# The adjacency is handed over with its last two axes swapped, and the gates' stage reads its tiles as loaded

## What is computed

```
h = relu(layernorm(x))
x_conv = conv branch of h (17 taps)
A   = exp(-dist(s, s)) * adj              # s = h @ w_se.T + b_se, 3 wide
msg = relu(h @ w_msg.T + b_msg)
x_nmp[n] = sum over m of A[n, m] * msg[m]
r, z, n = gates of [x_conv, x_nmp] and h  # the n gate: tanh(gi_n + r * gh_n)
x = x + (1 - z) * n + z * h
h2 = relu(layernorm(x))
out = x + relu(h2 @ w[:d] + (adj @ h2) @ w[d:] + bias)
```

## Time and profile before

| | us |
|---|---|
| median of 3 runs | 2045.76 |
| lowest and highest | 2044.67, 2048.74 |
| the profiled execution | 2044.45 |
| its span | 2042.6 |
| TensorE busy (matmuls) | 1902.4, 93% |
| VectorE busy | 1483.0, 73% |
| ScalarE busy | 797.3, 39% |
| POOL busy | 378.3, 19% |

### The profile page before, as it was taken

How to read it: one execution, slowest core, us unless ns; L and a number is a source line. 1 busy time by engine, 2 the same in 40 slices (tenths; PEclk the granted TensorE clock), 3 DMA queues, 4 the chain that set the end, 5 groups by cost and what they waited for, 6 DMA issues and landing times.

```text
span 2042.6 us, 37528 instructions
## 1 busy us (share of the span) xinstructions
PE 1902.4 (93%) x13018; PEld 1434.6 (70%) x13018; DVE 1483.0 (73%) x3288; ACT 797.3 (39%) x1478; POOL 378.3 (19%) x555
## 2 busy tenths in 40 slices
PE   2877989999975999999999999999999999999997
PEld 2566767764434777777777777787777777877775
DVE  3887878852234777877777778777777787777775
ACT  3864545544224333333333333333333333333332
POOL 1021111100012222221221222212212222122120
PEclk9999989999987999999999999999999999999998
DMA  2086565556234222322222223222222232222220
GB/s 99 12 295 231 193 217 193 198 215 249 98 140 146 71 82 68 97 74 74 96 68 87 83 68 99 71 74 96 68 92 79 68 100 70 76 94 68 91 79 16
DMA packets 162857, 224.40 MB, mean 110 GB/s; under 512 B 15863, under 2 KB 112878, under 8 KB 162030
## 3 DMA queue, kind: packets, MB, share of 16 engines
q1 hardware_dynamic: 162798, 223.62, 32.8%
HBM read 133.39 MB, written 90.18 MB: 109 GB/s over the span
## 4 chain that ended last, share of the span: by engine, by line
PE 63%; DVE 3%; ACT 2%; issue 0%; DMA 0%; POOL 0%; ACTq 0%; POOLq 0%; DVEq 0%
PE ps_rz L1241 26%; PE ps_n L1241 13%; PE ps_l L1241 13%; PE ps_b L1241 9%; DVE nmp L1347 2%; ACT nmp L1342 2%; PE ps_adj L1267 1%; PE ps_d L1250 1%; DMA rows<-spectra 0%; ACTq L1163 0%; PE ps_s L1201 0%; DVE sum_rz L1387 0%; POOL conv_x L1218 0%; POOL conv_v L1223 0%; PE ps_d L1465 0%
## 5 line engine op out<-in xcount | busy, mean ns | idle before, releaser
L1396 ACT ACTIVATE tanh_rz<-sum_rz,w_scale 128x512 f32<-128x512 f32 x128 | 92.5, 722 | 472.7 <-DVE sum_rz L1387 472.7
L832 PE MATMUL m_ps<-big 128*128 128x512 f16 (+1 forms) x1152 | 268.6, 376 | 5.1 <-DVE ysb L742 3.2
L1241 PE MATMUL ps_rz<-w_ih,nmp 128*128 128x512 f32 x768 | 206.1, 403 | 11.6 <-DVE nmp L1347 11.4
L1421 POOL TENSOR_TENSOR x_new<-xin,new 128x256 f32<-128x256 f32 x128 | 93.7, 732 | 662.6 <-ACT new L1414 662.6
L1241 PE MATMUL ps_rz<-w_ih,conv_t 128*128 128x512 f32 x768 | 209.3, 407 | 0.1
L832 PEld LDWEIGHTS m_ps<-big 128*128 128x128 f16 x1152 | 112.4, 98 | 109.7 <-DVE ysb L742 4.7
L1241 PE MATMUL ps_rz<-w_hh,ht 128*128 128x512 f16 x768 | 186.6, 379 | 0.9 <-DVE sum_n L1390 0.9
L1241 PE MATMUL ps_l<-w_l,h2t 128*128 128x512 f16 x768 | 179.1, 383 | 1.4 <-DVE h2t L1477 1.4
L1241 PEld LDWEIGHTS ps_rz<-w_ih,nmp 128*128 128x128 f32 x768 | 134.7, 188 | 50.6 <-DVE nmp L1347 26.7
L742 DVE SCALAR_TENSOR_TENSOR ysb<-m_ps,ysb 128x512 f16<-128x512 f32 x96 | 66.0, 689 | 119.8 <-ACT ysb L668 119.6
L1241 PEld LDWEIGHTS ps_rz<-w_ih,conv_t 128*128 128x128 f32 x768 | 134.8, 189 | 24.3 <-DVE conv_t L1233 0.3
(11 more groups left out here) (211 smaller groups left out, 3796.3 us busy)
## 6 DMA issues: line engine op xcount, KB each, us to landing
xin<-in_x SPq DMA_DIRECT2D x128, 256.0 KB, 2.9
spectra<-ysb SPq DMA_DIRECT2D x96, 256.0 KB, 2.0
rows<-spectra SPq DMA_DIRECT2D x64, 384.0 KB, 3.5
x_normed<-xhat SPq DMA_DIRECT2D x64, 256.0 KB, 3.4
h_turned<-ht SPq DMA_DIRECT2D x64, 256.0 KB, 2.5
adj_in<-in_adj SPq DMA_DIRECT2D x64, 256.0 KB, 3.7
ht<-h_turned SPq DMA_DIRECT2D x64, 256.0 KB, 3.3
xhat<-x_normed SPq DMA_DIRECT2D x64, 256.0 KB, 2.9
```

What stands on the lines that cost most here:

```text
L832: last = pe.matmul(dest, x_, w_, start=n == 0, stop=n == 11, skip_group_check=True)
L1241: last = pe.matmul(dest, stationary(dl), moving(wl), start=start and n == 0, stop=stop and n == 2, **kw)
L1396: act.activation(tanh_rz[:, i, :], sum_rz[:, i, :], ACT.Tanh, scale=w["scale"][:, 4:5]).then_inc(S["rz_tanh"], 1)
L1421: pool.tensor_tensor(x_new[:, i, :], xin[:, p, i, :], new[:, i, :], ALU.add).then_inc(S["x_new_done"], 1)
```

## The change

The host hands over the adjacency as adj[g, m, n] instead of adj[g, n, m], and the load puts m on the partitions: `adj_in[:, p, m, n]`. `turn_adj`, the tile ps_adj and the semaphore adj_turned are gone. `adj_split_high`, `adj_split_low` and `attention` read adj_in. `adj_split_high` and `attention` wait for the load, and the load of a buffer waits for `attention` and `adj_split_low` of the graph that had it, where it waited for the transposes.

```diff
-    adj_d = adj.rearrange("g (t p) m -> g p t m", p=P)
+    adj_d = adj.rearrange("g (m p) n -> g p m n", p=P)
...
-        ps_adj = ps("ps_adj")
...
         def load_rows(sp, t, p):
...
-            before(sp, "adj_turned", t, 1, 2)
+            before(sp, "att_done", t, 1, 2)
+            before(sp, "adj_low", t, 1, 2)
             sp.dma_start(adj_in[:, p, :, :], adj_d[t]).then_inc(adj_loaded[p], 16)
...
-        def turn_adj(pe, t, p):
-            arrived(pe, adj_loaded, t, p)
-            before(pe, "att_done", t)
-            before(pe, "adj_low", t)
-            for m in range(H):
-                for i in range(H):
-                    last = pe.transpose(ps_adj[:, m * N + i * P:m * N + i * P + P],
-                                        adj_in[:, p, i, m * P:m * P + P], ident[:, :])
-            last.then_inc(S["adj_turned"], 1)
-
         def adj_split_high(act, t, p):
-            ready(act, "adj_turned", t)
+            arrived(act, adj_loaded, t, p)
             before(act, "out_done", t, H, 2)
-            act.activation(adj_t[:, p, 0, :, :].rearrange("p h n -> p (h n)"), ps_adj[:, :],
-                           ACT.Copy).then_inc(S["adj_high"], 1)
+            act.activation(adj_t[:, p, 0, :, :], adj_in[:, p, :, :], ACT.Copy).then_inc(S["adj_high"], 1)
 
         def adj_split_low(dve, t, p):
             ready(dve, "adj_high", t)
-            dve.tensor_tensor(adj_t[:, p, 1, :, :].rearrange("p h n -> p (h n)"), ps_adj[:, :],
-                              adj_t[:, p, 0, :, :].rearrange("p h n -> p (h n)").bitcast(F32),
+            dve.tensor_tensor(adj_t[:, p, 1, :, :], adj_in[:, p, :, :], adj_t[:, p, 0, :, :].bitcast(F32),
                               ALU.subtract).then_inc(S["adj_low"], 1)
 
         def attention(dve, t, p):
             ready(dve, "exp_done", t)
+            arrived(dve, adj_loaded, t, p)
             before(dve, "att_high", t)
             before(dve, "att_low", t)
-            dve.tensor_tensor(att[:, :, :].rearrange("p h n -> p (h n)"),
-                              ps_adj[:, :], expd[:, :, :].rearrange("p h n -> p (h n)"),
-                              ALU.mult).then_inc(S["att_done"], 1)
+            dve.tensor_tensor(att[:, :, :], adj_in[:, p, :, :], expd[:, :, :], ALU.mult).then_inc(S["att_done"], 1)
...
                 def slot(t, p, prev, cur, nxt):
                     if cur:
-                        turn_adj(pe, t, p)
                         distances(pe, t, p)
...
-        value = np.ascontiguousarray(value)
+        value = np.ascontiguousarray(value.transpose(0, 2, 1) if name == "adj" else value)
```

More of the change, by code:

```diff
@@ L1147, in gates @@
         names = ("msg_done msg_added "
-                 "msg_high msg_low adj_turned adj_high adj_low dist_done exp_done att_done att_high att_low "
+                 "msg_high msg_low adj_high adj_low dist_done exp_done att_done att_high att_low "
                  "nmp_done nmp_high nmp_low conv_high conv_low rz_done n_done rz_added n_added rz_tanh "
```

## The result

The changed kernel takes 2051.86 us (median; 2050.64 to 2052.26) against 2047.02 for the kernel before on the same chip: a ratio of 1.0024 [1.0015, 1.0034]. On another chip, beside three of the experiments, it was 2052.54 against 2044.88, 1.0040 [1.0026, 1.0054]. So it is slower, by the medians 5 to 8 us, by the two intervals 0.15 to 0.54%. The forecast was 2053.2, 7.4 above the median of before that it was added to (2045.76).

A forecast was written before the change was run, and what follows sets the result against it. TensorE was taken to bound the gates' stage, with VectorE close behind. Even slots losing 0.19 us (30) and odd ones 0.05 (33) gave 7.4 us, added to the median 2045.76 for 2053.2 us; range 2041 to 2060.

The forecast's parts named there:

- What goes: TensorE before the weighted sum: of 0.44 us of transposes per slot, even slots keep 0.06 and odd ones 0.18.
- The sign given for it: TensorE idle some 0.3 to 0.45 us before the weighted sum, in a row that wasn't there before.
- adj_high: ScalarE's adj_high, ahead of exp: reading SBUF instead of PSUM makes the chain 0.05 us longer (0 to 0.07).
- The wait instruction: VectorE ahead of att, even slots only: 0.02 us taken, bounds nothing and 0.24, with 0.10 hidden at diff.
- the last rival: Wait ahead of att costs 0.24, shifting x_new and diff: some 0.17 us more in 30 slots, 2058 to 2061; chance 0.12.
- Beside POOL: adj_low's second SBUF source makes POOL's rstd sum and h2hat 0.37 us late, delaying nmp 0.12 in even slots.
- the prediction's first rival: POOL's two-element sum isn't held by adj_low: 4.3 us faster, 2041.5; chance 0.2.
- h2hat's turning "done before nmp": TensorE ahead of the gates: turning done 0.05 + 0.44 + 0.10 after h2hat's end, against 0.61 + 0.05 for nmp.
- The sum: Over 63 slots: 30 even ones lose 0.19 us and 33 odd ones 0.05, together 7.4 us slower.
- The second: Rival: TensorE keeps the whole 0.44 us per slot, 28.2 us faster, 2017.6; chance 0.04.
- The third: Rival: att's wait costs 0.24, so x_new and diff shift: 5 us more, 2058, up to 2061; chance 0.12.
- The fourth: Rival on the load: same size and row length, only the host's order differs, no price on the chip; no chance given.

The follow-up runs named there:

- the fourth experiment: The changed kernel without attention's own wait for the load, so no separate wait instruction stands ahead of att in even slots: 2050.46 us, ratio 1.0024.
- the first experiment: The kernel before with the four transposes made for graph 0 alone, all sources still in PSUM: 2037.98 us, ratio 0.9965.
- that of the second: The kernel before, transposes kept, with adj_low alone reading SBUF instead of PSUM: 2049.8 us, ratio 1.0021.

## Why the prediction was right

The time came within 1.4 us of the forecast by the first comparison (2051.86 against 2053.2), and +5 to +8 us by the two medians against +7.4. The time is off by less than the difference to before on that chip (4.8, off by 2.6), and that is luck: before's median of eight runs lies 1.3 above the median of three that the 7.4 was added to. The slots are the better test: 21.70 and 21.50 measured, 21.68 and 21.54 forecast. Point by point:

**What goes: right.** The gap before the weighted sum and the price of a hand-over are in the rows as worked out: msg ends at 1214.32 + 0.69 = 1215.01, TensorE starts at 1215.06 (0.05), and the twelve matmuls take 1.70 where they took 1.59 (0.11). Run alone, the term was 0.05 and 0.15 where 0.06 and 0.18 were forecast. The sign given for it, TensorE idle for 0.3 to 0.45 before the weighted sum, was too large: 0.22 in even slots and 0.02 in odd ones. The weighted sum starts 6.48 after sum_rz where it started 6.52 after, so 0.40 of the 0.44 is waited out there, but 0.16 of that doesn't show as idle time, because before the change the matmuls' rows overlapped by 1210.52 + 0.86 - 1211.22 = 0.16:

```profile
1210.52 0.86 PE L1241 MATMUL ps_n<-w_ih,conv_t 128*128 128x256 f32 x6
```


**adj_high: a little under.** It takes 0.61 from SBUF, between 577 and 630 ns and nearer to the upper; exp ends 0.03 later on the chain, not 0.05. In the odd slots msg ends 1236.51 - 1232.38 - 4.10 = 0.03 late.

**The wait instruction: mis-sized.** The step took 0.02 for it. It cost 0.20 (att 0.23 after exp, 0.03 without it), near the bound of 0.24 from POOL's row, and that row was the one to take. The second half of the step was right in kind: diff took 0.42 instead of 0.53, so some of it was hidden, and msg ends 1215.01 - 1211.01 - 3.88 = 0.12 late where 0.07 stood. Of the 0.12, 0.03 is adj_high and 0.09 this; taken out alone, in the fourth experiment, it gave 0.13, as diff then took 0.49 and not 0.53. x_new grew from 0.73 to 0.79 behind the later att, a little of what the last rival feared and not enough to shift diff.

**Beside POOL: right, and the term that decides.** The sum took 0.55 (0.5 to 0.6), VectorE idled 0.87 before h2hat (0.9), and h2hat started 1217.01 - 1212.65 - 3.88 = 0.48 late in the even slot, which is the 0.12 of the chain and 0.36 of POOL's (0.37). nmp started 0.08 before h2hat's end, as the step had it, 0.22 late. The rule of the Trainium skill in "SBUF — State Buffer", "Who interferes with whom", holds here down to an operation of two columns, which the prediction's first rival doubted: with adj_low's source the only edit the sum went from 0.20 to 0.55.

**h2hat's turning "done before nmp": only just.** The step had 0.05 + 0.44 + 0.10 for it against 0.66 for nmp. The turning began 0.06 after h2hat's end and nmp's matmuls 0.60 after that, at 1218.40, 0.05 after nmp's end at 1218.35. It is a tie, and the trace puts the wait on h2hat (0.17) and none on nmp, where I had foretold more than 0.2 before nmp. The time is the same by either.

**The sum.** Even slots +0.21 (0.19 foretold): the chain brought 0.12 instead of 0.07, and POOL's hold and h2hat's own duration were 0.01 each under their rows (0.36 for 0.37, 0.73 for 0.74), with rounding for the rest. Odd slots +0.01 (0.05 foretold): 0.03 instead of 0.05 through the chain, less the same two hundredths. 30 x 0.21 + 33 x 0.01 = 6.6 against 7.4, and 6.8 measured.

**The rivals.** The first fell by the rstd row. The second fell by the first experiment and by the transposes put back, which cost nothing. The third was half right: its wait instruction was there and its shift of x_new was not, as its hold is 0.06. The fourth held: a load of adj_in lands 3.6 us after its issue in the median, where it was 3.7 before.

What stays open: no run removed adj_high's 0.03 alone, the median of the fourth experiment can't confirm the 3 us that its profile shows, and that of the second lies 2 us above what its profile shows.

## What to carry to other kernels

TensorE's 63% of the span on the chain that ended last was no proof that its work is worth its time: what bounds is seen where its next dependent input arrives, and here VectorE was 0.2 to 0.3 us behind it. Work that stands in a wait is free and its removal is worth the gap alone, so look before moving or deleting it at what it covers. When an operand moves from PSUM to SBUF, look which POOL instruction is issued while that instruction runs, however small it is, and place the instruction elsewhere; and count the waits on each instruction, as one too many becomes an instruction of its own on the chain. When two chains share an engine, the order in which they interleave is part of their price: each can fill the other's gaps.

## What the hardware showed that was not expected

- A wait instruction of its own ahead of a VectorE instruction costs 0.20 us when the awaited event has yet to come (att 0.23 after exp against 0.03).
- POOL's sum on 128x2 is held as fully as a wide instruction, from 0.20 to 0.55, until 1215.64 + 0.55 - 0.20 = 1215.99 by its own duration: 0.15 before adj_low's end at 1216.14, the same 0.15 as x_new had beside diff.
- A ScalarE copy of 128x512 takes 613 ns from SBUF and 577 from PSUM, same output.
- Stages that no edit touched came to the last `w_bias_msg` row between 639.98 and 642.91 us in twelve profiles, so a difference of two spans can be off by some 2 or 3 us until the common part is taken off.
